# Startup of a four-layer transformer kernel: constants fetched in the order of first use, the first projections put into the loading block, a constant row written once

## The reference

```
xn = layernorm(x)
x  = x + sequence_part(xn) * silu(feed_forward(xn))
```

## Time and profile before

| what | value |
|---|---|
| median of 3 runs | 4093.51 us (4087.54 to 4095.2) |
| the profiled execution: its own time | 4094.77 us |
| the profiled execution: span of instructions | 4093.0 us |
| PE busy | 3463.2 us, 85% of the span |
| DVE busy | 2559.0 us, 63% |
| ACT busy | 1771.9 us, 43% |
| POOL busy | 969.6 us, 24% |
| mean granted PE clock | 0.966 |
| DMA traffic | 140.05 MB in the whole span |

### The profile page before, as it was taken

One profiled execution on the slowest core, in us unless ns is written; L12 is line 12 of the kernel. 1 busy time (PEld: TensorE's weight loads), 2 busy tenths in 40 slices (PEclk: granted clock), 3 DMA queues, 4 the chain that ended last, 5 costly groups with the idle time before them and its releaser, 6 DMA issues. The chain is left out here.

```text
span 4093.0 us, 56361 instructions
## 1 busy us (share of the span) xinstructions
PE 3463.2 (85%) x19826; PEld 1800.6 (44%) x19983; DVE 2559.0 (63%) x5512; ACT 1771.9 (43%) x3774; POOL 969.6 (24%) x809
## 2 busy tenths in 40 slices
PE   3988888888988889888988889888888889888867
PEld 1344444444344443444344443444434443444434
DVE  3567665666566655666656665566556666566655
ACT  1544434443444534444344434435254444444314
POOL 1023311323023310332113320223103331132214
PEclk9999999999999999999999999999999999999978
DMA  4000010001011020000101020010100001110230
GB/s 159 22 21 27 29 39 32 25 13 61 6 32 37 1 67 29 15 27 33 35 32 34 5 67 1 32 37 1 67 32 11 27 33 35 32 35 4 67 83 22
DMA packets 87846, 140.05 MB, mean 34 GB/s; under 512 B 12472, under 2 KB 62466, under 8 KB 85002
## 3 DMA queue, kind: packets, MB, share of 16 engines
q1 hardware_dynamic: 79250, 124.15, 9.5%
q10 hardware_dynamic: 8314, 12.21, 1.0%
HBM read 106.14 MB, written 29.39 MB: 33 GB/s over the span
## 5 line engine op out<-in xcount | busy, mean ns | idle before, releaser
L635 DVE TENSOR_REDUCE nmax<-banks 128x1 f32<-128x512 f32 (+3 forms) x1216 | 760.9, 658 | 412.9 <-PE banks L448 209.6
L558 ACT ACTIVATE probs<-banks 128x512 f32<-128x512 f32 (+3 forms) x1024 | 475.7, 527 | 290.7 <-PE banks L467 202.7
L448 PE MATMUL banks<-ks,qs 72*128 72x512 bf16 (+3 forms) x1536 | 446.3, 336 | 89.4 <-DVE nmax L635 60.6
L467 PE MATMUL banks<-qs,ks 74*128 74x512 bf16 (+3 forms) x1536 | 448.0, 333 | 45.3 <-ACT probs L558 17.2
L97 PE MATMUL banks<-filler,identb 128*128 128x512 bf16 x1632 | 423.2, 388 | 26.3 <-PEq L77 18.9
L448 PEld LDWEIGHTS banks<-ks,qs 72*128 72x128 bf16 x1536 | 142.3, 99 | 376.0 <-DVE nmax L635 214.1
L558 ACT ACTIVATE early<-banks 128x256 f32<-128x256 f32 (+3 forms) x512 | 195.2, 440 | 174.4 <-PE banks L467 171.5
L97 PEld LDWEIGHTS banks<-filler,identb 128*128 128x128 bf16 x1776 | 172.1, 99 | 220.9 <-issue 77.0
L1514 ACT ACTIVATE probs<-banks,nm 128x192 f32<-128x192 f32 x512 | 172.1, 421 | 213.5 <-DVE nm L1466 213.5
L517 PE MATMUL banks<-probs,v 128*32 128x512 f32 (+3 forms) x2048 | 235.3, 531 | 20.4 <-DVE att L622 10.3
L1548 POOL TENSOR_TENSOR probs<-probs,inv 128x768 f32<-128x768 f32 x128 | 187.0, 1466 | 253.6 <-DVE inv L1476 253.6
(11 more groups left out here) (484 smaller groups left out, 6672.8 us busy)
## 6 DMA issues: line engine op xcount, KB each, us to landing
qs<-parts_scratch SPq DMA_DIRECT2D x300, 96.0 KB
ks<-parts_scratch SPq DMA_DIRECT2D x288, 96.0 KB
parts_scratch<-parts SPq DMA_DIRECT2D x50, 384.0 KB, 2.5
shared<-in_w_h SPq DMA_DIRECT2D x17, 1024.0 KB, 7.6
shared<-in_w SPq DMA_DIRECT2D x25, 256.0 KB, 3.0
qs<-max_parts SPq DMA_DIRECT2D x192, 4.0 KB
xn<-in_x SPq DMA_DIRECT2D x9, 256.0 KB, 2.7
factor_scratch<-g SPq DMA_DIRECT2D x9, 256.0 KB
```

The costliest lines, as they stand in the source:

```text
L448: mm = nc.tensor.matmul(K.ps[:, b, i * keys:(i + 1) * keys], K.qs[0:72, 4 * g + j, t * P:(t + 1) * P], K.ks[0:72, 4 * g + j, 0:keys], star ...
L467: mm = nc.tensor.matmul(K.ps[:, b, q0:T], K.ks[0:KR, h, k * P:(k + 1) * P], K.qs[0:KR, h, q0:T], start=True, stop=not on_tensor)
L558: nc.scalar.activation(probs[:, 4 * (q % QUADS) + m % 4, q0:T], K.ps[:, bank("second", m), q0:T], ACT.Exp, scale=scale).then_inc(exped, 1)
L635: nc.vector.tensor_reduce(nmax[:, t, h:h + len(heads)], K.ps[:, n % 2, 0:len(heads) * keys].rearrange("p (j k) -> p j k", k=keys), AX.X, A ...
```

## The change

- The loads are sorted into more lists by first use: `shown` (x of sample 0), `projects` (identity, projection weights, biases, rotary tables and two scales), `gates` (the two weights of the first gated step), `tables` (local-attention tables, scales, masks), `first` (fp4 weights), `soon` (the rest of layer 0), `late`. `late` is cut: 16 loads on SP and 12 on ACT go out early, the last 8 of each behind the spread loads.
- The three blocks become one. In it DVE normalises, builds the tables, runs its part of `NextQkv`, and only then rounds the fp4 weights; PE runs `NextQkv` and then turns the weights. The end of the block waits for `soon` as before.
- POOL writes `neghalf` and `v` first, then takes the power, then fills 32 partitions of `ks` (64 to 95, 8192 bf16 elements each) with ones. The spread loads wait for this, and overwrite rows 64 to 71.
- `ones_d`, its store, and the load of ones in every quad are gone; a quad waits for six loads.
- The scratch of the rotary step is the fp4 scratch tile, since both now live in one block; `ks` and `qs` are allocated ahead of the block.

```diff
@@ spread_loads
-        if keys:
-            engine.dma_start(K.ks[72:74, heads, :], K.ones_d[:, heads, :]).then_inc(K.spread[g], 16)
@@ attention, on PE
-                        pe.wait_ge(K.spread[g], 7 * 16)
+                        pe.wait_ge(K.spread[g], 6 * 16)
@@ batch_loop, the loading block
             @block.sync
             def _(sp):
-                for loads, landed in ((first, first_landed), (soon, soon_landed), (late, K.late_landed)):
-                    for dst, src in loads[0::2]:
-                        sp.dma_start(dst, src).then_inc(landed, 16)
-                sp.wait_ge(filled, 1)
-                sp.dma_start(K.ones_d, ones[:, :, :]).then_inc(K.factor_stored, 16)
-                sp.wait_ge(K.factor_stored, 16)
-                sp.wait_ge(soon_landed, 16 * len(soon))
+                fetch(sp, shown, shown_in)
+                fetch(sp, projects[2::2], projects_in)
...
+                fetch(sp, first[0::2], first_in)
+                fetch(sp, soon[0::2], soon_in)
+                fetch(sp, late[0:16], K.late_landed)
+                nxt.store_parts(sp)
+                sp.wait_ge(ones_set, 1)
+                spread_loads(nc, K, sp, keys=False)
+                fetch(sp, late[28::2], K.late_landed)
+                sp.wait_ge(soon_in, 16 * len(soon))
             @block.scalar
             def _(act):
...
+                fetch(act, tables[0:1], tables_in)
+                nxt.run(nxt.on_scalar, nxt.TURN)
+                fetch(act, first[1::2], first_in)
+                fetch(act, soon[1::2], soon_in)
+                fetch(act, late[16:28], K.late_landed)
+                act.wait_ge(projects_in, 16 * len(projects))
+                nxt.run(nxt.on_scalar)
+                act.wait_ge(ones_set, 1)
+                spread_loads(nc, K, act, queries=False)
+                fetch(act, late[29::2], K.late_landed)
             @block.gpsimd
             def _(pool):
-                nc.gpsimd.memset(ones[:, :, :], 1.0).then_inc(filled, 1)
...
+                next_power(nc, K, pool)
+                pool.wait_ge(K.pool[66], 1)
+                nc.gpsimd.memset(K.ks[64:96, :, :], 1.0).then_inc(ones_set, 1)
+                pool.wait_ge(ones_set, 1)
                 nc.gpsimd.memset(K.filler[:, :], 1.0)
             @block.vector
             def _(dve):
...
-                dve.wait_ge(first_landed, 16 * len(first))
+                dve.wait_ge(shown_in, 16 * len(shown))
+                normalise_next(nc, K, dve, nxt.normed)
+                dve.wait_ge(tables_in, 16 * len(tables))
...
+                nxt.run(nxt.on_vector)
+                dve.wait_ge(first_in, 16 * len(first))
                 quantize_weights(nc, K, w4, q4, scr, ch, quantized)
             @block.tensor
             def _(pe):
+                pe.wait_ge(projects_in, 16 * len(projects))
+                pe.wait_ge(nxt.normed, NT)
+                nxt.run(nxt.on_tensor)
+                pe.wait_ge(nxt.h_ready, 4)
                 pe.wait_ge(quantized, 1)
...
-    first_projections(nc, K)
```

More of the change, by code:

```diff
@@ L1877, in normalise_next @@
     for t in range(NT):
[L1878 to L1879 removed]
+        scaled = nc.vector.tensor_scalar(K.xr[:, t, :], K.xn[:, t, :], K.mv[:, t, 0:1], K.rstd[:, t:t + 1],
+                                         ALU.subtract, ALU.mult)
+        if normed:
+            scaled.then_inc(normed, 1)
 def next_power(nc, K, pool):
@@ L2433, in x_tiles @@
         return A["x"][b, :, :].rearrange("(t p) d -> p t d", p=P)
-    first, soon, late = [], [], []
+    shown, projects, gates, tables, first, soon, late = [], [], [], [], [], [], []
     def whole(name, src=None, bc=False, loads=late):
@@ L2445, in whole @@
         return t
-    K.w0_qkv = whole("w0_qkv", loads=soon)
-    K.b0_qkv = whole("b0_qkv", bc=True, loads=soon)
+    K.w0_qkv = whole("w0_qkv", loads=projects)
+    K.b0_qkv = whole("b0_qkv", bc=True, loads=projects)
     shared = sb("shared", [P, 11 * T])
@@ L2455, in batch_loop @@
         (t, A[n][:, :, :]) for t, n in ((K.w0_h1, "w0_h1"), (K.w0_h2, "w0_h2"), (K.w0_3, "w0_3"))]
-    soon.extend(K.w0_loads)
+    gates.extend(K.w0_loads[0:2])
+    soon.extend(K.w0_loads[2:])
     K.late_qT, K.late_kT = K.w0_h1, K.w0_h2
     late_v = [shared[:, (8 + t) * T:(9 + t) * T] for t in range(NT - 1)]
-    K.s0_1, K.s0_2, K.s0_h1, K.s0_h2 = [whole(n, loads=soon) for n in ("s0_1", "s0_2", "s0_h1", "s0_h2")]
+    K.s0_1, K.s0_2 = [whole(n, loads=projects) for n in ("s0_1", "s0_2")]
+    K.s0_h1, K.s0_h2 = [whole(n, loads=soon) for n in ("s0_h1", "s0_h2")]
     K.s0_3 = whole("s0_3", bc=True, loads=soon)
@@ L2487, in batch_loop @@
     cos, sin = rope_tables()
-    K.rope_cos = whole("rope_cos", nc.inline_tensor(cos, name="rope_cos_c").ap(), loads=soon)
-    K.rope_sin = whole("rope_sin", nc.inline_tensor(sin, name="rope_sin_c").ap(), loads=soon)
+    K.rope_cos = whole("rope_cos", nc.inline_tensor(cos, name="rope_cos_c").ap(), loads=projects)
+    K.rope_sin = whole("rope_sin", nc.inline_tensor(sin, name="rope_sin_c").ap(), loads=projects)
     K.iota8 = whole("iota8", nc.inline_tensor(np.arange(E3, dtype=np.float32), name="iota8_c").ap(), bc=True)
@@ L2518, in batch_loop, with fetch @@
         first.append((w4[:, :, :].rearrange("p c d -> p (c d)")[:, 6 * D:6 * D + I1], A["w_downr"]))
-        first.append((K.ident[:, :], nc.inline_tensor(np.eye(P, dtype=np.float32), name="ident_c").ap()))
-        first.append((ct[:, :], nc.inline_tensor(consts, name="masks_c").ap()))
-        first.append((tabs[:, :, :, :], nc.inline_tensor(xpos_tables(), name="xpos_c").ap()))
-        first.append((qks[:, :, :, :], A["qk_scales"].partition_broadcast(P)))
         K.late_loads = len(late)
         turns = weight_turns(K, q4)
-        first_landed, soon_landed, filled, vec, pvec, quantized, turned, copied = K.pool[0:8]
+        (shown_in, projects_in, gates_in, tables_in, first_in, soon_in, ones_set, v_set, half_set, vec, pvec, quantized,
+         turned, copied) = K.pool[0:14]
+        nxt = NextQkv(nc, K, tmp, gates_in, sines).start(nc)
+        def fetch(engine, loads, landed):
+            for dst, src in loads:
+                engine.dma_start(dst, src).then_inc(landed, 16)
         with nc.Block() as block:
@@ L2561, in _ @@
                     ch.do(nc.vector.memset(pad, 1.0))
-                dve.wait_ge(first_landed, 16 * len(first))
+                dve.wait_ge(shown_in, 16 * len(shown))
+                normalise_next(nc, K, dve, nxt.normed)
+                dve.wait_ge(tables_in, 16 * len(tables))
+                for L in range(2):
+                    for m, t in enumerate((K.cosq[L], K.sinq[L], K.cosk[L], K.sink[L])):
+                        nc.vector.tensor_tensor(t[:, :, :], tabs[:, m, :, :],
+                                                qks[:, L, m, :].unsqueeze(1).to_broadcast([P, NT, LD]), ALU.mult)
+                dve.wait_ge(projects_in, 16 * len(projects))
+                dve.wait_ge(v_set, 1)
+                nxt.run(nxt.on_vector)
+                dve.wait_ge(first_in, 16 * len(first))
                 quantize_weights(nc, K, w4, q4, scr, ch, quantized)
@@ L2568, in _ @@
                     o += n
-                for L in range(2):
-                    for m, t in enumerate((K.cosq[L], K.sinq[L], K.cosk[L], K.sink[L])):
-                        nc.vector.tensor_tensor(t[:, :, :], tabs[:, m, :, :],
-                                                qks[:, L, m, :].unsqueeze(1).to_broadcast([P, NT, LD]), ALU.mult)
                 dve.wait_ge(turned, len(turns))
```

72 lines of the change are left out of this document (25 added, 47 removed).

## The result

The changed kernel takes 4103.01 us (median of 14 runs, 4096.21 to 4109.51), before in the same runs 4093.49 (4085.53 to 4101.38): ratio 1.0027, 95% interval [1.0019, 1.0034]. It is slower by 9.5 us; 4068 was predicted. The profiled execution took 4096.21 us, its span 4094.5.

The account below looks back on a forecast made before the run. The prediction took the start, the serial chain to the first score matmul at 80.55 us, as the bound. First scores at 55.2 gain 25.4 us, the loop 0: from the median 4093.51 to 4068 us, range 4057 to 4081.

Parts of the forecast that it names:

- x landed: Start: x, now the first load on SP's queue, issued at about 0.8 us, taken as landed at 3.8 us.
- `xr` held by the fill: Start: DVE's four scalings of x wait for POOL's fill of ones and end at 14.7 us instead of 7.5.
- the second rival: Start: the fill holds nobody up; first scores at 49.5, 31 us gained, 4062.5 us; chance 0.17.
- parts from: First block: ACT, delayed 0.65 us by issuing 17 loads, starts the parts at 29.0 us.
- store issued: First block: SP issues the parts store at 31.8 us and goes on 3.5 us later if its queue is drained.
- the third rival: Start: queues take over, parts store stuck behind 29 loads; scores at 62.9, 17.6 us gained, 4076 us; chance 0.16.
- fp4 done: First block: DVE finishes the fp4 weights, now behind the gated products, at 53.2 us, as the last engine.
- ACT's end: First block: ACT issues twelve `ks` loads and eight constants after its last activation, ending at 49.0 to 51.6 us.
- The fourth rival: First attention: constants set back stop it; no change, or 4103 us if landing near 120; chances 0.04 and 0.03.
- eight late constants 3.6 to 8.85 us: First block: SP's eight constants behind twelve spread loads take 3.6 to 8.85 us; SP ends at 47.6 to 52.9.
- the 25.4: Whole start: first scores at 55.2 us instead of 80.55, so 25.4 us gained.
- in the loop: I take 0: Loop over samples: 96 removed loads of ones gain between 0 and 2.4 us; 0 taken.

Follow-up runs that it names:

- fill_later: Changed kernel with POOL's fill of `ks` waiting until x is normalised, so behind the four scalings of x: 4092.7 us.
- late_early: Changed kernel with SP's eight last constants issued ahead of the store of the parts instead of behind the spread loads: first scores at 58.56 us.
- loop_only: Kernel before with only the loop's part of the change, the ones rows of `ks` loaded once ahead of the loop: 4094.8 us.
- padded: Changed kernel with long-fulfilled waits added in its first block, 7 to 15 instructions per engine: 4091.7 us, 4024.7 from the first scores.
- both_padded: Changed kernel with the edits of late_early and fill_later together, plus the added waits of padded: 4076.7 us, 4024.9 from the first scores.
- both_padded_dram: both_padded with the unused DRAM scratch of the ones declared again: 4068.35 us, ratio 0.9948 [0.9930, 0.9965].
- before_shift: Kernel before with 49 to 57 long-fulfilled waits per engine added in its first block: 4093.7 us against 4089.1 beside it.
- after_again: Changed kernel measured once more, unchanged, for a second trace: 4101.6 us.

## Why the prediction was wrong

Right, with what was measured: x landed at 3.7 us (3.8); `rstd` at 6.4 (6.4); `xr` held by the fill to 14.1 (14.7), shown by fill_later, so the second rival is out; parts from 27.7 (29.0); store issued at 30.5, and the first spread load 4.3 us behind it (31.8, 3.5), so the third rival's mechanism, a store stuck in the queue, did not come (in fill_later, where the parts are stored earlier, it did: 8.4 us); fp4 done at 52.0 (53.2); ACT's end 52.2 (49.0 to 51.6). The fourth rival is out: the first maxima are stored at 95.25, 29.2 us after the first scores, 29.8 before.

**First failed step: "eight late constants 3.6 to 8.85 us".** They took 20.9 (43.65 to 64.55). Both bounds came from places where nothing slow stood ahead on the queue; here twelve spread loads did. late_early put them elsewhere, and they took 6.0. That step cost 11 us of the 25.4 (14.5 were gained), and it was the end of SP, not of DVE, that set the first scores, as in the third rival for another reason.

**Second failed step: "in the loop: I take 0", bounds 0 and -2.4.** It was +24 us. Most of it is time at the lower clock: the median clock is 0.957 against before's 0.967 in the later sets, some 82 us more at the lower level, of which the traces put 18 into the start; the other 64 are worth 21 to 23 us. The busy times of DVE, ACT and POOL behind the first scores moved by 1.5 us at most over the whole run, and the exit from the loop adds 1.7. loop_only shows that the removed loads alone have no part in it. What has is where things stand: padded gave back 8 to 12 us by added waits that move the code and do no work (twice, with both_padded), less than half of it through the clock (0.957 to 0.9585 and 0.959, some 12 to 16 us less at the lower level, worth 4 to 6); the tensor declared ahead of two others gave another 9 to 13 on top (twice), through the clock. Neither works everywhere: with ten fillers the waits give nothing back, and without the waits the tensor doesn't. With both, the time from the first scores on is 4014 to 4016, at the old kernels' 4009 to 4015, so the new start itself leaves nothing behind. The prediction took it for granted that identical code runs in identical time, and had no rival for the opposite.

Of the sum: 80.55 - 25.4 = 55.2 was reached, and passed, only in the versions with both edits (51.8 to 52.9), and only both_padded_dram shows it in the time: 28.4 us earlier at the scores, and by its ratio 0.0052 x 4091 = 21 us in all.

**What stays open.** How the place of the code or of a DRAM tensor comes to change the mean clock and, for the code, the waits inside the loop. The traces show barrier waits that move by 0.3 to 0.4 us with the place of the code, a loop exit that is 1.7 us longer when instructions are fetched in it, and samples that repeat exactly in one of several forms (474.5, 477.9, and in padded 471.2 next to 481.0). Why a kernel mostly falls into a dearer form isn't settled: a shorter sample went with it in the changed kernel, but before_shift is as short and doesn't pay. The price of the lower clock is from its agreement with the time, at 0.32 to 0.36 us per us; no run set it by itself.

## What to carry to other kernels

Price a moved DMA issue by what stands ahead of it on its queue at the new place: the same eight loads took 6 us ahead of the spread loads and 20.9 behind, though half of that gain was lost again to other issues beside them. Put a long fill behind, not beside, the scalings that the next stage waits for. Before a small gain at the start is given up as a loss, look at how the granted clock of the untouched part moved, and try other places for code and tensors; a range for a change of 0.5% should hold some 25 us for that here.

## What the runs showed of the hardware

- A wait at a barrier depends on where its code stands: 1.42 or 1.80 us, 5.72 or 7.43, for the same instructions.
- The wait behind the loop is 7.3 to 7.5 us in the nine traces with two instruction transfers on q14 in its last 3.4 us, and 5.7 in the eleven without.
- The loop's samples can repeat to 0.03 us. Two fillers more in each, 3.4 us of work in all, cost 10 us in two kernels and nothing that shows in a third.
- After the same work of PE (13.92 and 5.81 us busy in 16.0 and 7.3) one kernel's clock fell to 0.50 and the other's stayed at 1.00.
- Over the runs of one kernel time follows the mean granted clock: after_again 4086.8 us at 0.962, 4100.3 to 4103.2 at 0.957, 4109.2 at 0.954.
- A single issue on a hardware queue can hold its engine for 7.96 us (SP, behind the spread loads) or 5.76 us (ACT in late_early, behind constants alone).
- Four scalings on DVE from SBUF to SBUF take 7.70 us beside a fill on POOL and 1.12 without; DVE products of two SBUF tiles take 0.42 us beside the same fill.
